# One core, mixer, attention and experts in one kernel: where the first-layer expert weights are folded, how the zero key enters the denominators, and the order of the work

## The reference, cut to what matters

```
zf, zi, zh = x @ Wf + bf, x @ Wi + bi, x @ Wh + bh        # gated recurrence, in logs
log_h = a_star + cumlogsumexp(log_val - a_star)            # 257 steps: the first is log 0.5
h = exp(log_h)                                             # (8, 257, 128)

h = h + attention(layernorm(h))     # 8 heads of 16; keys and values of the other batch half
                                    # softmax over all 257 keys
xf = layernorm(h)
shared and 16 routed experts: he = xf @ w1 + b1
g = clip(he[..., ::2]); u = clip(he[..., 1::2])
t = g * sigmoid(g * alpha) * gate_scale * (u + up_shift)
out = h + sum_over_top2(cw * (t @ w2 + b2)) + shared(t @ w2 + b2)
```

## Time and profile before

| | |
|---|---|
| median of 3 runs | 304.44 us |
| the profiled execution | 303.86 us |
| its span, first to last instruction | 302.0 us |
| mean granted TensorE clock | 0.945 |
| TensorE busy | 275.3 us |
| VectorE busy | 239.7 us |
| ScalarE busy | 188.6 us |
| GpSimd busy | 118.4 us |

### The profile page before, as it was taken

How to read it: one execution, slowest core, us unless ns; L and a number is a source line. 1 busy time by engine, 2 the same in 40 slices (tenths; PEclk the granted TensorE clock), 3 DMA queues, 4 the chain that set the end, 5 groups by cost and what they waited for, 6 DMA issues and landing times.

```text
span 302.0 us, 5217 instructions
## 1 busy us (share of the span) xinstructions
PE 275.3 (91%) x1766; PEld 167.0 (55%) x1766; DVE 239.7 (79%) x421; ACT 188.6 (62%) x298; POOL 118.4 (39%) x84
## 2 busy tenths in 40 slices
PE   2994996689989999989999999999979999999993
PEld 1421343446546775554676685447748659767641
DVE  1096645997499989889999699999887977689991
ACT  2849698969768766643688954636877485325051
POOL 2002546480041586063009176200943920391920
PEclk9995798579999999999999999999999996899998
DMA  6800000000000000000010000000000100000011
GB/s 226 358 0 0 0 1 1 2 0 2 2 0 4 0 2 0 0 3 0 2 36 3 0 2 2 0 0 3 0 2 1 37 0 2 1 0 0 2 35 35
DMA packets 3373, 5.78 MB, mean 19 GB/s; under 512 B 266, under 2 KB 2450, under 8 KB 3218
## 3 DMA queue, kind: packets, MB, share of 16 engines
q1 hardware_dynamic: 3348, 5.46, 5.0%
HBM read 4.40 MB, written 1.05 MB: 18 GB/s over the span
## 4 chain that ended last, share of the span: by engine, by line
PE 75%; DVE 11%; issue 7%; ACT 5%; DMA 1%; POOL 0%; DVEq 0%; SPq 0%; ACTq 0%; POOLq 0%
PE bank L1146 73%; DVE mxt L901 3%; PE bank L1149 2%; DVE tr L998 1%; DMA cst<-in_consts 1%; DVE yr L966 1%; ACT qt L635 1%; DVE tr L1018 1%; DVE qt L912 1%; DVE vr L976 1%; ACT pt L672 1%; DVE yo L1028 0%; ACT z L575 0%; ACT al L601 0%; DVE mxt L907 0%
## 5 line engine op out<-in xcount | busy, mean ns | idle before, releaser
L523 POOL TENSOR_TENSOR vr<-vr,cwb 128x1024 f32<-128x1024 f32 x24 | 63.3, 2652 | 16.5 <-DVE vr L976 14.0
L1146 PE MATMUL bank<-tr,w 128*128 128x512 f32 (+1 forms) x104 | 47.8, 599 | 0.0
L901 DVE TENSOR_REDUCE mxt<-bank 128x2 f32<-128x512 f32 x64 | 40.4, 685 | 9.3 <-PE bank L1146 9.0
L724 ACT ACTIVATE tr<-yr,fpar 128x1024 f32<-128x1024 f32 (+1 forms) x28 | 30.1, 1088 | 26.1 <-PE bank L1146 14.1
L1146 PE MATMUL bank<-xh,w1h 128*128 128x512 f32 x104 | 46.3, 446 | 0.0
L966 DVE TENSOR_SCALAR yr<-bank,fpar 128x512 f32<-128x512 f32 x52 | 39.4, 801 | 5.8 <-PE bank L1146 5.7
L1146 PE MATMUL bank<-xh,w1l 128*128 128x512 f32 x104 | 41.5, 400 | 0.0
L1146 PE MATMUL bank<-xl,w1h 128*128 128x512 f32 x104 | 41.5, 399 | 0.0
L998 DVE SCALAR_TENSOR_TENSOR tr<-tr,yr 128x1024 f32<-128x1024 f32 (+1 forms) x28 | 36.6, 1324 | 5.3 <-ACT tr L724 5.3
L672 ACT ACTIVATE pt<-bank 128x512 f32<-128x512 f32 x64 | 33.8, 602 | 9.1 <-PE bank L1146 9.1
L517 POOL TENSOR_SCALAR vr<-vr,fpar 128x1024 f32<-128x1024 f32 x12 | 15.2, 1267 | 48.6 <-ACT vr L711 48.6
(11 more groups left out here) (182 smaller groups left out, 431.9 us busy)
## 6 DMA issues: line engine op xcount, KB each, us to landing
pt<-in_w1a SPq DMA_DIRECT2D x1, 1672.0 KB, 9.2
xt<-in_x SPq DMA_DIRECT2D x4, 256.0 KB, 7.4
out<-osb SPq DMA_DIRECT2D x8, 128.0 KB, 1.9
w<-in_w SPq DMA_DIRECT2D x1, 832.0 KB, 10.7
...
out<-zo SPq DMA_DIRECT2D x1, 4.0 KB
```

What stands on the lines that cost most here:

```text
L523: g.tensor_tensor(vr[:, n % NV, :, :], vr[:, n % NV, :, :], cwb[:, u % 2, :].unsqueeze(1).to_broadcast([P, 2, W]), ALU.mult).then_inc(S["v ...
L724: a(halves(k, tr, n % NT), halves(k, yr, n % NY), ACT.Tanh, scale=fpar[:, HA, r:r + 1]).then_inc(S["th"], 1)
L901: last = v.tensor_reduce(top_of, ps.bank("mx", u, s, c, t)[:, :].rearrange("p (i t) -> p i t", i=2), AX_X, ALU.max)
L1146: return nc.tensor.matmul(out_, lhsT, rhs, start=start, stop=stop, **k)
```

## The change

- The raw weights are loaded without row 0, which comes by a transfer of its own with the new one-row input of shifts (in `pt`, behind the weights). The original row 0 is repeated on all partitions on the host (zeros on partition 0) and loaded into all of `tr` (1.71 MB instead of 26 KB).
- VectorE adds the shifts to the up columns of row 0 (`w1s`, one partition, 1664 elements), subtracts `tr` from the raw weights in place (`w1p`, seven parts) and makes the router weights (`gw`). ScalarE's `w1h` and VectorE's `w1l` read SBUF instead of PSUM. `wp` and the selector `bsel` are gone.
- The zero key's product `o0` (one f32 product, 128 columns of weights by 256) becomes four products of 32 weight columns each at the head of `pv` for block 0, and is no piece of its own.
- A half (`g` or `u`) waits for `xl` only in the first half of its unit (`FIRST_HALF`), and for the weights only in unit 0, on one semaphore; `zg` waits for one semaphore instead of seven banks.
- `AT` and `BANK_OF` are new. TensorE's order now begins `z` of units 0 and 1, `lsum.1`, `lsum.0`, `center.0.1`, `var.0.1`, `lsum.2`, `z.2.1`, `v.0`, `q.0`, `z.2.0`, `z.2.2`, `k.0`, `mx.0.0.0`, `mx.0.0.1`, `z.3.0`, `z.3.2`, `nmt.0.0`, `z.3.1`, `lsum.3`, `st.0.0.0`, `st.0.0.1`, `mx.0.1.0`, `center.1.1`, `mx.0.1.1`, `pv.0.0.0`, `var.1.1`, `nmt.0.1`, `pv.0.0.1`, `st.0.1.0`, `k.1`, `st.0.1.1`, `q.1`. VectorE's begins with unit 0's recurrence, `h1.0`, `w1s`, `gw`, `xn.0.1`, `w1p.0`, `l.1`, `w2s`, `w1p` 1 to 6, `w1l` 0 and 1, `w.1`, `mscan.1`, `dw.1`, the eight `mr` of half 0, `mz`, `w1l.2`, `nm.0.0`, `w1l.3`, `l.2`, `w1l.4`, `w.2`, `w1l` 5 and 6, `mscan.2`, `sscan.1`, `dw.2`, `xsum.0` and the eight `mr` of half 1. TensorE's order now ends `down.3.1`, `g.3.11`, `zg` 0 to 5, `down.3.2`, `zg` 6 to 9, `down.3.3`, `zg` 10 to 12, `down.3.4`, `down.3.5`, `down.3.6`, `out.3`, `zd`, `zout`; VectorE's ends `te.3.6`, `zclip`, `yo.3`, `zgg`, `zte`, `zy`.

```diff
-SETUP_PIECES = [(n, 0, k) for k in range(W1_PARTS) for n in ("wp", "w1h", "w1l")] + [("w2s", 0)]
+SETUP_PIECES = [("w1s", 0)] + [(n, 0, k) for k in range(W1_PARTS) for n in ("w1p", "w1h", "w1l")] + [("gw", 0), ("w2s", 0)]
...
+FIRST_HALF = [next(p for p in order("P") if p[0] in "gu" and p[1] == u) for u in range(UNITS)]
...
-            sp.dma_start(w1_raw, w1a_in).then_inc(s_w1a, 16)
+            sp.dma_start(w1_raw[0:1, :], w1a_in[0:1, :]).then_inc(s_shift, 16)
+            sp.dma_start(shift, shift_in.rearrange("p (c n) -> p c n", n=P)).then_inc(s_shift, 16)
+            sp.dma_start(w1_raw[1:P, :], w1a_in[1:P, :]).then_inc(s_w1a, 16)
             sp.dma_start(w1_row, w1b_in).then_inc(s_w1b, 16)
...
             def w1h_(u, k):
-                ps.filled(act, "wp", 0, k)
-                n = w1_part(k).stop - w1_part(k).start
-                a(w1h[:, w1_part(k)], ps.bank("wp", 0, k)[:, 0:n], ACT.Copy).then_inc(s_w1h, 1)
+                act.wait_ge(s_w1p, k + 1)
+                a(w1h[:, w1_part(k)], w1_raw[:, w1_part(k)], ACT.Copy).then_inc(s_w1h, 1)
...
+            def w1s(u):
+                dve.wait_ge(s_shift, 32)
+                up_rows = w1_raw[0:1, 0:W1COLS].rearrange("p (c k n) -> p c k n", k=2, n=P)[:, :, 1, :]
+                v.tensor_tensor(up_rows, up_rows, shift, ALU.add).then_inc(s_w1s, 1)
+
+            def w1p(u, k):
+                dve.wait_ge(s_w1a, 16)
+                dve.wait_ge(s_w1b, 16)
+                dve.wait_ge(s_w1s, 1)
+                v.tensor_tensor(w1_raw[:, w1_part(k)], w1_raw[:, w1_part(k)], w1_row[:, w1_part(k)], ALU.subtract).then_inc(s_w1p, 1)
+
             def w1l_(u, k):
                 dve.wait_ge(s_w1h, k + 1)
-                n = w1_part(k).stop - w1_part(k).start
-                if k == W1_PARTS - 1:
-                    v.tensor_copy(gate_w[:, :], ps.bank("wp", 0, k)[:, n:n + E]).then_inc(s_gw, 1)
-                last = v.tensor_tensor(w1l[:, w1_part(k)], ps.bank("wp", 0, k)[:, 0:n], w1h[:, w1_part(k)].bitcast(F32), ALU.subtract)
-                ps.release(last, "wp", 0, k)
+                v.tensor_tensor(w1l[:, w1_part(k)], w1_raw[:, w1_part(k)], w1h[:, w1_part(k)].bitcast(F32), ALU.subtract)\
+                    .then_inc(s_w1l, 1)
...
-            def wp(u, k):
-                pe.wait_ge(s_const, 16)
-                pe.wait_ge(s_w1a, 16)
-                pe.wait_ge(s_w1b, 16)
-                ps.take(pe, "wp", 0, k)
-                cols = slice(k * W, min((k + 1) * W, W1COLS + E))
-                o = ps.bank("wp", 0, k)[:, 0:cols.stop - cols.start]
-                mm(o, ident, w1_raw[:, cols], stop=False)
-                ps.fill(mm(o, const("bsel")[0:2, :], w1_row[:, cols], start=False), "wp", 0, k)
...
-            def o0(u, s):
-                ps.released(pe, "nmt", u, s)
-                ps.take(pe, "o0", u, s)
-                ps.fill(mm(ps.bank("o0", u, s)[:, T:W], const("e0sel"), e0[:, s, :], start=True, stop=False, skip_group_check=True),
-                        "o0", u, s)
-
             def pv(u, s, c):
...
+                if c == 0:
+                    ps.released(pe, "nmt", u, s)
+                    ps.take(pe, "o0", u, s)
+                    for t in range(PAIRS):
+                        last = mm(o[32 * t:32 * t + 32, T:W], const("e0sel")[:, 32 * t:32 * t + 32], e0[:, s, :], start=True, stop=False,
+                                  skip_group_check=True)
+                    ps.fill(last, "o0", u, s)
...
             def half_(u, c, name, kind):
-                ge(pe, "xl", u + 1)
-                for k in sorted({(2 * c + kind) * P // W, ((2 * c + kind + 1) * P - 1) // W}):
-                    ps.released(pe, "wp", 0, k)
+                if not AT or (name, u, c) == FIRST_HALF[u]:
+                    ge(pe, "xl", u + 1)
+                if u == 0:
+                    pe.wait_ge(s_w1l, ((2 * c + kind + 1) * P - 1) // W + 1)
```

More of the change, by code:

```diff
@@ L34 @@
 for _name, _n in (("wtok", 3 * P), ("btok", 3), ("omat", P), ("cmat", P), ("wq", P), ("wk", P), ("wv", P), ("ident", P),
-                  ("head", 2), ("row", 2), ("nrow", 2), ("ones32", 64), ("e0sel", P), ("bsel", P), ("b2s", 1), ("par", 10)):
+                  ("head", 2), ("row", 2), ("nrow", 2), ("ones32", 64), ("e0sel", P), ("b2s", 1), ("par", 10)):
     CONSTS[_name] = (_at, _at + _n)
@@ L69, in unit_pieces @@
             a += [("st", u, s, c)] + [("pt", u, s, c, t_) for t_ in range(PAIRS)]
-            a += [("o0", u, s)] * (c == 0) + [("pv", u, s, c)]
+            a += [("pv", u, s, c)]
         a += [("den", u, s), ("on", u, s), ("h2", u, s)]
@@ L203, in filled_by @@
         return [("y0", u)]
+    if name == "pv":
+        return [("o0", u, numbers[0])] if numbers[1] == 0 else []
     if name == "zg":
         return [("zg", 0)] if numbers[0] == 0 else []
-    one_bank = ("wp", "z", "lsum", "center", "var", "q", "k", "v", "nmt", "o0", "gate", "cwb", "g", "u", "out",
+    one_bank = ("z", "lsum", "center", "var", "q", "k", "v", "nmt", "gate", "cwb", "g", "u", "out",
                 "zv", "zc", "zvar", "zgate", "zcw", "zd", "zout")
@@ L243, in release, with build @@
         instruction.then_inc(self.free[self.place[key][0]], 1)
-def build(nc, x_in, consts_in, w1a_in, w1b_in, w2_in, out):
+def build(nc, x_in, consts_in, w1a_in, w1b_in, shift_in, w2_in, out):
     ctx = ExitStack()
@@ L318, in build @@
         w1_raw = pt[:, :, :, :].rearrange("p a b c -> p (a b c)")[:, 0:W1COLS + E]
-        w1_row = tr[0:2, :, :, :].rearrange("p a b c -> p (a b c)")[:, 0:W1COLS + E]
+        w1_row = tr[:, :, :, :].rearrange("p a b c -> p (a b c)")[:, 0:W1COLS + E]
+        shift = pt[0:1, :, :, :].rearrange("p a b c -> p (a b c)")[:, W1COLS + E:W1COLS + E + NC * P].rearrange("p (c n) -> p c n", n=P)
         memory = [ctx.enter_context(nc.psum_tensor(f"bank{i}", [P, 512], F32)) for i in range(BANKS)]
@@ L668, in pt_ @@
                 if u == 0 and s == 0:
-                    for k in range(W1_PARTS):
-                        ps.filled(act, "wp", 0, k)
+                    act.wait_ge(s_w1l, W1_PARTS)
+                    act.wait_ge(s_gw, 1)
                 ge(act, "pv", n - NPT + 1)
@@ L718, in th @@
                 if u == 0:
-                    for j in range(W1_PARTS):
-                        ps.filled(act, "wp", 0, j)
+                    act.wait_ge(s_w1l, W1_PARTS)
+                    act.wait_ge(s_gw, 1)
                 clipped(act, "g", GATE_BY, n, "gcv", "gcg")
@@ L1135, in _ @@
             dve.wait_ge(s_bias, BIASES)
-            run("V", {"w1l": w1l_, "t": t_, "d": d_, "hg": hg, "l": l_, "w": w_, "mscan": mscan, "dw": dw,
+            run("V", {"w1s": w1s, "w1p": w1p, "w1l": w1l_, "gw": gw, "t": t_, "d": d_, "hg": hg, "l": l_, "w": w_, "mscan": mscan, "dw": dw,
                       "sscan": sscan, "lf": lf, "h1": h1_, "h2": h2, "xn": xn, "xsum": xsum, "mr": mr, "mz": mz,
@@ L1339, in zg @@
                 ge(pe, "zsplit", 2)
-                for k in range(W1_PARTS):
-                    ps.released(pe, "wp", 0, k)
+                pe.wait_ge(s_w1l, W1_PARTS)
                 if c == 0:
@@ L1370, in _ @@
             run("P", {"z": z_, "lsum": lsum, "center": center, "var": var, "q": q_, "k": k_, "v": v_, "mx": mx, "nmt": nmt,
-                      "st": st, "o0": o0, "pv": pv, "gate": gate, "cwb": cwb_, "g": gate_half, "u": up_half, "down": down,
-                      "out": out_, "zv": zv, "zc": zc, "zvar": zvar, "zgate": zgate, "zcw": zcw, "zg": zg, "zd": zd, "zout": zout, "wp": wp})
+                      "st": st, "pv": pv, "gate": gate, "cwb": cwb_, "g": gate_half, "u": up_half, "down": down,
+                      "out": out_, "zv": zv, "zc": zc, "zvar": zvar, "zgate": zgate, "zcw": zcw, "zg": zg, "zd": zd, "zout": zout})
 def layout(inputs):
@@ L1405, in layout @@
     shift = features(np.repeat(sa[2], I), np.repeat(ea[:, 2:3], I, axis=1))
-    shift = np.stack([np.zeros_like(shift), shift], axis=1).reshape(-1)
-    w1b = np.stack([w1[0], np.concatenate([shift, np.zeros(E, np.float32)])])
+    w1b = np.repeat(w1[0:1], P, axis=0)
+    w1b[0] = 0.0
+    shift = shift.reshape(1, -1)
     w2e, w2s = f("L0_ffn_expert_w2")[:, :, perm], f("L0_ffn_shared_w2")[:, perm]
@@ L1431, in layout @@
         "ident": eye, "head": at, "row": row, "nrow": -row,
-        "bsel": bsel, "ones32": np.concatenate([zero16, one16, one16, zero16], axis=1), "e0sel": e0sel,
+        "ones32": np.concatenate([zero16, one16, one16, zero16], axis=1), "e0sel": e0sel,
         "b2s": f("L0_ffn_shared_b2")[perm][:, None], "par": par,
@@ L1435, in layout @@
     consts = np.concatenate([parts[n] for n in CONSTS], axis=1)
-    arrays = {"x": x, "consts": consts, "w1a": w1a, "w1b": w1b, "w2": w2.reshape(P, -1)}
+    arrays = {"x": x, "consts": consts, "w1a": w1a, "w1b": w1b, "shift": shift, "w2": w2.reshape(P, -1)}
     return {k: np.ascontiguousarray(a) for k, a in arrays.items()}
```

13 lines of the change are left out of this document (7 added, 6 removed), and 100 rows, old and new, of tables (AT, BANK_OF, BY).

## The result

The changed kernel takes **357.07 us** (median of 4 runs, 356.69 to 362.17), the kernel before 304.93 beside it (4 runs): ratio **1.1743** [1.1682, 1.1804]. The forecast was 295.0 with a range up to 302.5, and a chance of 0.76 for faster. The profiled execution took 356.78 us with a span of 354.8, TensorE busy 76% of it and VectorE 71%, at a mean granted clock of 0.869.

A forecast was written before the change was run, and what follows sets the result against it. TensorE, busy 91% of the span and 75% of the chain, was taken as the bound, with VectorE to watch. 303.86 - 6.7 - 0.8 - 3.3 + 3.9 - 3.0 + 1.0 = 295.1, given as 295 us; range 289.5 to 302.5.

The forecast's parts named there:

- Step 1, the loads: Opening loads: 1.69 MB more, 4.7 us more for what queues behind on SP, taken at 0 with 10 us of slack.
- Step 1, the lead of 6.7 us: Start: folding steps leave TensorE, so work through unit 0's scores runs 6.7 us ahead, bounds 1.7 and 8.
- The recurrence's 1.7: Start, within the lead: the first center product begins at 25.5 us instead of 27.2, 1.7 us gained.
- the clock stays low through the start: Rival, chance 0.12: without filler products TensorE runs at clock 0.50 from 25.5 to 64 us, costing 4 us: 299.
- only filler: Rival, chance 0.15: the removed wp products at the start were only filler, the lead shrinks to 1.7 us: 303.
- Step 2: Zero key in 32-column products at the head of pv: -0.8 us, between -1.6 and +0.8.
- Step 3: Fewer waits on TensorE's halves: taken as 0, at most 4.9 us.
- Step 4: First row's work: zd and zout move behind out.3, -3.3 us in the dense part, +3.9 us at the end.
- Step 5: Clock near 252 us: zg in groups between down products removes the loss at 0.50, -3.0 us (0 to -3.4).
- Step 6: Rest of the new order, moving halves, down and attention steps among each other: +1.0 us.

The follow-up runs named there:

- one_load: The changed kernel with the raw weights loaded by one transfer of 128 rows, the shifts alone staying a transfer of their own: 309.09 us, ratio 1.0149.
- one_load_filler: one_load with eight extra 128x512 products on TensorE, results unused, placed in its idle time: 301.73 us, ratio 0.9916.
- the filler runs: Eight extra unused TensorE products added to one_load, and to the changed kernel loading row 0, 7 and 120 rows separately: 301.73 and 300.08 us.
- fold_only: The kernel before with only the fold moved to VectorE, raw weights in one load, old order, zero-key product and waits kept: 312.11 us, ratio 1.0227.
- zero_key_and_waits: The kernel before with only the zero key as four 32-column products inside pv and the fewer waits: 309.91 us, ratio 1.0173.
- whole_in_pv: The kernel before with the whole 128-column zero-key product moved to just ahead of pv: 309.33 us, ratio 1.0161.
- zg_spread: The kernel before with its eleven zg pieces moved from ahead of gate.3 to between unit 3's first halves: 316.08 us, ratio 1.0377.
- wide_between_zg: The kernel before with three extra 128x512 products, results unused, among the zg pieces: 308.5 us, ratio 1.0124.
- rows_7_120_timed: The changed kernel with raw weights as three transfers (row 0, rows 1 to 7, rows 8 to 127), in rounds: 308.38 us, ratio 1.0091.

## Why the prediction was wrong, step by step

**Step 1, the loads: failed, 48.0 us.** The sentence that failed is "Two small loads are put ahead (about 0.4 us of issue each)", with "0, with 10 us of slack". I priced volume, 1.69 MB at the 362 GB/s of the opening, and issue time, and never asked what cutting off one row does to the transfer of the other 127. The loads that come later were priced rightly: one_load brings the same 1.69 MB in time. No row of before shows a transfer of an odd shape; this was an unshown cost, to be bounded, and I gave it no upper bound. That `gw` waits for it ahead of `xn` in VectorE's order turned a late load into a standstill.

**Step 1, the lead of 6.7 us: failed.** The recurrence's 1.7 came (first `center` at 25.87 for 25.5). From `nm.0.0` to `nm.0.1` it took 22.1 us in one_load and 17.2 with TensorE filled (50.76 to 67.96), where I counted 15.1: VectorE's queue with no wait for TensorE. In one_load it waits 1.09 and 1.60 us for the score products ahead of the second half's maxima, with filler 0.68. `mz`, 278 ns in the mean before, shows 746 in one_load (groups of instructions):

```profile
L927 DVE TENSOR_SCALAR mxt<-mxt 128x16 f32<-128x16 f32 x8 | 6.0, 746 | 0.2
```

`st.0.1.1`, at 72.54 before, begins at 75.86 in one_load: behind, not 6.7 us ahead. With filler it begins at 71.94. Each `mz` that takes over 0.2 us in before, one_load and one_load_filler ends within 0.1 us of the end of a GpSimd step beside it; alone it takes 0.15 to 0.18. I had no term for that. Of the 7.0 us missed between the two `nm`, 4.9 go when TensorE is filled (`mz` included), and 2.1 stay unexplained.

**The rival "the clock stays low through the start"** (0.12, priced at 4 us) is what the filler runs bear out, at 7.4 us. It is so only in part: from 28 to 76 us one_load spends 20.7 us at the lower level, the kernel before 19.0. My sum had the products from `nm.0.0` on at no cost, since VectorE's queue was to cover them. The argument I set against it, that VectorE's queue and not TensorE ends last there, is refuted: no product was taken away, only added. The page I had cited with it, "TensorE: Matmul & The Clock Gate" in the Trainium skill, section "Why this matters for your kernels", speaks against long gaps between bursts, and the filled runs agree with it. Here the lower level also came behind waits of 1.66 and 0.73 us (one_load, 92 us) and behind none (before, 251.7 us). I weighed it as a cost of the start alone, though one_load loses the clock again at 92 us. The rival "only filler" had the right object, the early `wp`; what these were worth as filler was not measured, since fold_only also moved work on VectorE.

**Step 2: size right, its place missed.** The new form costs 0.45 us where I had 0.44 (timeline of one_load):

```profile
65.93 0.64 PE L1166 MATMUL bank<-e,cst 128*32 128x256 f32 x8
66.38 1.05 PE L1166 MATMUL bank<-pt,vpad 128*32 128x256 f32 x16
```

That the product also moves behind a wait I did not follow; in the old order that place costs 1.6%. What it costs in the new order was not measured. **Step 3: 0 fits**: zero_key_and_waits and whole_in_pv differ by less than their intervals.

**Step 4: the end is right.** From `yo.3` (297.98) to the end, 307.2, are 9.2 us in one_load, 9.3 forecast, with `zd` between its two prices, as the clock falls under it (0.68 in the last stretch below). The parts I listed add up to 8.1 and 11.0, not 8.3 and 11.2. That the dense part got 3.3 us shorter was not measured by itself:

```profile
298.78 0.66 PE L1169 MATMUL bank<-cst,yo 128*128 128x128 f32 x4 [1.34 <-DVE yo L1048]
299.79 4.34 PE L1166 MATMUL bank<-zy,w 128*128 128x8 f32 x26 [0.36 <-DVE zy L1124]
```

```profile
252.00:256.00 4.00, 3.89 (x18) 2.33 (x17) 3.96 (x10) 2.64 (x4) 0.52 (x1) 1.00 0.00 0
299.79:304.10 4.31, 4.31 (x26) 4.24 (x26) 0.00 (x0) 0.77 (x1) 0.00 (x0) 0.68 0.22 61
```

**Step 5: the row came, the reason is doubtful.** The clock is 1.00 at 252 in one_load, the first of the stretches above. But the `zg` pieces before were also the cover of a 4.5 us wait (zg_spread), and a few wide products among them do not keep the clock (wide_between_zg). That narrow products as such cost the clock is not shown: the 24 that stand in a row from 283.1 to 285.8 us in one_load run at 1.00, and under the same 24 in rows_7_120_timed it falls (0.76 from 280 to 284).

**Step 6 and what stays open.** The steps add up to 295.0, not the 295.1 of the sum. With transfer and start mended, 301.7 stands against it. About 4 us of the 6.7 can be seen at `nm.0.1` (67.96 for 64.0). The rest is in the order, or was never there; nor was it tried what the new order gives with the zero key's product ahead of the waits.
